# Reciprocal behind its guard, contiguous broadcast reads and a shorter lag in the query phase of a convolution, attention and expert-routing kernel

## The reference

```python
q = jax.nn.elu(q) + 1.0
k = jax.nn.elu(k) + 1.0
kv_cos = jnp.einsum('bshx,bshz->bhxz', k_cos, v)          # and kv_sin
qkv = jnp.einsum('bshx,bhxz->bshz', q_cos, kv_cos) + ...   # the same with sin
denom = 1.0 / (jnp.einsum('bshd,bhd->bsh', q_cos, k_cos.sum(axis=1)) + ... + 1e-05)
o = qkv * denom[..., None]
concat = o.reshape(b, s, h * d)
return concat @ dense_w.T + dense_b
```

## Time and profile before

| | us |
|---|---|
| median of three runs | 3816.84 |
| lowest, highest | 3796.03, 3817.02 |
| profiled execution | 3805.87 |
| its span | 3804.1 |
| PE busy | 3269.6 (86%) |
| DVE busy | 2955.0 (78%) |
| ACT busy | 1744.9 (46%) |
| POOL busy | 1609.1 (42%) |
| DVE idle until an `RB` load landed | 164.7 |

### The profile page before, as it was taken

One profiled execution on the slowest core, in us unless ns is written; L12 is line 12 of the kernel. 1 busy time (PEld: TensorE's weight loads), 2 busy tenths in 40 slices (PEclk: granted clock), 3 DMA queues, 4 the chain that ended last, 5 costly groups with the idle time before them and its releaser, 6 DMA issues.

```text
span 3804.1 us, 50603 instructions
## 1 busy us (share of the span) xinstructions
PE 3269.6 (86%) x16676; PEld 1503.9 (40%) x16676; DVE 2955.0 (78%) x3282; ACT 1744.9 (46%) x1880; POOL 1609.1 (42%) x1078
## 2 busy tenths in 40 slices
PE   4698888988898887988889888988889888998876
PEld 3343344433443334433444334433354334443353
DVE  6887977889787986879778896879878796758723
ACT  1166524764356533665247643565346642443210
POOL 1067712865147721676128650477217661210000
PEclk8899999999999998999999999999999999999967
DMA  1002640055201551025400552015510353106645
GB/s 51 18 1 60 136 98 27 1 119 119 65 19 27 132 119 44 1 65 132 96 27 1 119 118 65 19 25 133 119 44 1 79 126 89 32 1 138 138 124 214
DMA packets 154850, 279.55 MB, mean 73 GB/s; under 512 B 30285, under 2 KB 149613, under 8 KB 149677
## 3 DMA queue, kind: packets, MB, share of 16 engines
q1 hardware_dynamic: 154557, 275.89, 30.4%
HBM read 242.78 MB, written 33.05 MB: 73 GB/s over the span
## 4 chain that ended last, share of the span: by engine, by line
PE 46%; DVE 21%; DMA 14%; issue 9%; ACT 4%; SPq 3%; POOL 1%; DVEq 1%; ACTq 0%; POOLq 0%
DMA RB<-r_keep 10%; PE ps_C L1466 9%; PE ps_B L1451 5%; PE ps_A L1451 5%; PE ps_D L1466 4%; PE ps_E L1466 4%; DVE region L1112 4%; DMA r_keep<-RR 3%; DVE region L1104 3%; PE ps_D L1533 3%; DVE arena L930 3%; PE ps_D L1319 3%; PE ps_C L1533 2%; PE ps_E L1512 2%; DVE RR L1132 2%
## 5 line engine op out<-in xcount | busy, mean ns | idle before, releaser
L587 POOL TENSOR_TENSOR arena<-arena,UHL 128x896 f32<-128x896 f32 x525 | 1179.5, 2255 | 405.9 <-ACT UHL L719 404.1
L1112 DVE TENSOR_TENSOR region<-region,RB 128x896 f32<-128x896 f32 x448 | 615.9, 1375 | 165.2 <-DMA RB<-r_keep 164.7
L719 ACT ACTIVATE UHL<-arena,W8C 128x896 f32<-128x896 f32 x525 | 542.1, 1033 | 0.0
L565 POOL TENSOR_SCALAR ST<-ST 128x14 f32<-128x14 f32 x64 | 28.8, 449 | 1121.4 <-DVE ST L985 1119.5
L755 ACT ACTIVATE EQ<-ps_B,NEG 128x896 f32<-128x896 f32 x224 | 225.6, 1007 | 496.4 <-PE ps_B L1495 496.4
L1533 PE MATMUL ps_C<-region,small 128*128 128x448 f32 x896 | 408.5, 584 | 22.4 <-DVE region L1112 22.4
L1533 PE MATMUL ps_D<-region,small 128*128 128x448 f32 x896 | 395.8, 566 | 37.0 <-DVE region L1112 37.0
L597 POOL TENSOR_TENSOR UA<-region,CS 128x128 f32<-128x128 f32 (+1 forms) x400 | 229.4, 575 | 415.1 <-PE ps_C L1466 365.8
L1466 PE MATMUL ps_C<-region,UA 128*128 128x512 f32 (+1 forms) x800 | 378.4, 595 | 1.4 <-ACT region L653 1.3
L930 DVE SCALAR_TENSOR_TENSOR arena<-arena,W8C 128x448 f32<-128x448 f32 (+1 forms) x243 | 365.2, 1526 | 0.0
L755 ACT ACTIVATE EQ<-ps_A,NEG 128x896 f32<-128x896 f32 x224 | 225.4, 1006 | 270.5 <-PE ps_A L1495 270.5
(11 more groups left out here) (294 smaller groups left out, 5115.3 us busy)
## 6 DMA issues: line engine op xcount, KB each, us to landing
RB<-r_keep SPq DMA_DIRECT2D x448, 448.0 KB, 6.2
arena<-x SPq DMA_DIRECT2D x8, 1568.0 KB, 7.5
t_keep<-Y SPq DMA_DIRECT2D x7, 1568.0 KB, 5.2
r_keep<-RR SPq DMA_DIRECT2D x448, 7.0 KB, 2.1
w_keep<-region SPq DMA_DIRECT2D x7, 784.0 KB, 5.9
CST<-t_keep SPq DMA_DIRECT2D x2, 1568.0 KB, 9.8
small<-t_keep SPq DMA_DIRECT2D x2, 1568.0 KB, 13.3
plane<-w_keep SPq DMA_DIRECT2D x4, 784.0 KB, 16.1
```

Source lines behind the costliest of these rows:

```text
L587: pool.tensor_tensor(out=X[:, cut], in0=X[:, cut], in1=PRODUCT[m % 3], op=ALU.add).then_inc(pool_taps.sem, 1)
L719: act.activation(PRODUCT[m % 3].rearrange("p (h w) -> p h w", w=W), g_window(2 * g * ROWS + 2 * (k // 5), 2 * (k % 5) - 4, 2 * ROWS), ACT. ...
L1112: dve.tensor_tensor(out=q, in0=q, op=ALU.mult, in1=RB[:, cc].rearrange("p (c n) -> p c n", c=2)).then_inc(scaled.sem, 1)
```

## The change

Four edits, which all serve one ordering. `RECIP_LAG` goes from 6 to 5, so the reciprocal stands directly behind the guard. The lags of scaling, output, parts and fold each go down by one slot, and the slots of the second token norm with them; the phase has 69 slots instead of 70. The token transposes stand in even slots now, in which `ps_A` holds a projection, so they take `ps_B`. The columns of `SEL` are permuted so that the 16 rows of `r_keep` are kept by partition half (8 rows for i = 0, then 8 for i = 1), and each load then reads four neighbouring rows, one run of 7168 B per partition, where it read four runs of 1792 B.

```diff
-DEN_LAG, SUM_LAG, RECIP_LAG, RB_LAG, OUT_LAG, PARTS_LAG, FOLD_LAG = 4, 5, 6, 10, 11, 15, 20
+DEN_LAG, SUM_LAG, RECIP_LAG, RB_LAG, OUT_LAG, PARTS_LAG, FOLD_LAG = 4, 5, 5, 9, 10, 14, 19
...
-LN2_SLOTS = {29: 0, 45: 1, 61: 2, 69: 3}
-ALL_SLOTS = 70
+LN2_SLOTS = {28: 0, 44: 1, 60: 2, 68: 3}
+ALL_SLOTS = 69
...
-                uses += [(("yt2", LN2_SLOTS[j]), "A")] if j in LN2_SLOTS else []
+                uses += [(("yt2", LN2_SLOTS[j]), "BA"[j % 2])] if j in LN2_SLOTS else []
...
-                            at = HEADS * (s % 2) + 8 * h + i
-                            sp.dma_start(RB[HALVES[i], 2 * h:2 * h + 2, :].rearrange("p b (c n) -> p (b c) n", n=PIX),
+                            at = HEADS * (s % 2) + NCHUNK * i + 4 * h
+                            sp.dma_start(RB[HALVES[i], 2 * h:2 * h + 2, :].rearrange("p b n -> p (b n)"),
...
-                                                 [[0, C], [2 * PIX, 4], [1, PIX]]))\
+                                                 [[0, C], [1, 4 * PIX]]))\
...
-            link(dve.tensor_tensor(out=SEL[:, 0:HEADS].rearrange("p (g c h) -> p g c h", g=2, h=2),
+            link(dve.tensor_tensor(out=SEL[:, 0:HEADS].rearrange("p (h g c) -> p g c h", g=2, h=2),
```

## The result

The changed kernel is slower by half a per cent: 1.0055 of the time before, with an interval of 1.0044 to 1.0067. The medians are 3807.98 us before (15 runs, among them the three shown above) and 3826.9 after (15 runs). The ratio makes 17 to 26 us more, where the forecast was 3 us less than before. The profiled execution has a span of 3820.8 us against 3804.1, 16.7 more.

The account below looks back on a forecast made before the run. The DRAM loop of reciprocal, store, load and scaling was taken as the bound. Per turn +0.45 - 0.20 - 0.25 = 0.0; per pair +0.76 - 0.89 - 0.2 = -0.3, -3 us for 8 pairs: 3814, range 3762 to 3860.

Parts of the forecast that it names:

- The bound: Middle query step: the loop reciprocal, store, load, scaling, next reciprocal, 12.78 us, binds; DVE and PE aren't full.
- The intervals with the token norm: Four of 13 reciprocal intervals per pair, bound by DVE: guard's turn adds 0.76 us per pair, moved norm nothing.
- PE as the bound: Rival: PE waits 0.7 us per turn at the denominators' first half, +50 us, 3867; chance 0.17.
- The load: Loads of `RB` in the loop, longer runs: gain 0.2 us per turn, ends +0.25 and -0.4.
- The faster-load rival: Long runs bring a pair of `RB` loads 1 us sooner: -57 us in all, 3760; chance 0.23.
- The guard: On DVE it comes into the loop between scaling and reciprocal: +0.45 us per turn, lower end 0.26.
- The store: Stores of the reciprocals come through faster since half 1 loads start earlier: 0.25 us gained per turn, at worst nothing.
- First reciprocal and packets: Each pair's first reciprocal starts 0.89 us sooner; DMA packets fall by 86,016 if each run is one packet.
- Signs that were given for a wrong forecast: Landing under 5.6 us, a second L1512 wait in each turn, or token-norm intervals changing by more than 1 us.

Follow-up runs that it names:

- runs_only: Kernel before with the change's `SEL`, `r_keep` and loads (7168 B runs), old lags kept: 3781.83 us, -22 against before.
- scale_runs: Changed kernel with `RECIP_LAG` back at 6, so the reciprocal stands behind the second scaling of the step before: 3968.61 us, +164 against before.
- before_shortpool: Kernel before with each of POOL's convolution additions cut to 56 of 896 columns, rest of the sum left out: 3680.06 us, -123 against before.
- runs_only_den3: runs_only with PE's first half of the denominators one slot later: 3846.03 us, +39 against before.
- lags_only: Kernel before with the change's lags, slots and transposes' area, but old row order and 1792 B runs: 3863.88 us, +61 against before.
- recip_runs: runs_only with the reciprocal one slot up (slot 4s+5), all other lags as before: 3727.70 us, -77 against before.

## Why the prediction was wrong

**The bound: the failing step.** "Neither is full, the loop is the bound" took PE's 11.71 and DVE's 11.64 busy us as slack of one us in each, and DVE's wait of 1.14 as time that only a shorter loop would change. What the runs showed: with a shorter load the 3rd to 6th turns stay at 12.8 us, because the scaling grows by what the wait loses (0.95 + 1.38 before, 0.24 + 2.09 in runs_only). With a feature and a scaling more in the loop they go to 15.3 (scale_runs), and with POOL's additions shortened they fall to 12.4 (before_shortpool). A part of DVE's busy time is scalings of 2 us beside an addition that take 1.08 without one; it isn't a fixed amount of work that leaves slack. In the changed kernel the load's wait fell by 70 us, DVE's busy time grew by 39, and the sum over terms of the loop had neither.

**The intervals with the token norm: a term near nothing.** The sum gave the four intervals that don't wait for a load 0.76 us per pair, and to the token norm, moved with the lags, it gave "I count nothing". In the third pair these are the 7th, 8th, 10th and 11th. By the medians they changed by -0.9, +2.4, +0.3 and +1.7, together 3.4 us per looped pair before rounding, and some 24 for seven. That alone turns the forecast of 3 us less into a loss. In the 8th, L997 now stands ahead of a feature job that PE waits for. The distance that the prediction called kept is that of the transposes and their area; it didn't look at this part of the norm.

**PE as the bound: a rival that came true in part.** It put a wait of 0.7 us at the first half of the denominators into each of nine turns, 50 us in all. That half waits in three steps of a looped pair, by 1.08 to 1.23 us; its waits grew from 6.9 to 27.0 us in the whole kernel. The wait of 1.07 that the rival took from the earlier trace rows belongs to the second half, and those waits didn't grow (127.2 and 126.6). That moving the first half gives back 47 us is more than its own wait; the move also fills waits of the second.

**The load: sized too low.** 0.2 us per turn were taken, from a range up to 0.4; the landing of a load fell by 0.4, and by 0.5 in runs_only (6.2 to 5.7). The estimate of 0.2 to 0.3 us, worked out from the Trainium skill's "DMA: Bandwidth & Descriptors", section "Why small descriptors are slow (HBM only)", was for a pair of loads, and the landings lie above it. The reading that long runs are no faster where 64 partitions are the target is refuted. It rested on two rates from stretches that also hold other transfers. The prediction drew the same from the 8 of 16 ports that the Trainium skill, "SBUF — State Buffer", section "Door 1: The DMA port swizzle", gives partitions 0 to 63; that section says nothing of the length of a run, and no run here tests the ports. What the gain is worth depended on what else bound: 22 us in the old order, about 40 in the new lags, 53 with the loop open, 64 without the additions. The faster-load rival (3760) named the right mechanism and still gave too much, since in the old order half of the wait it removed (33 of 66 us) turned into longer scalings.

**The guard: nearly right in size, wrong in worth.** 0.45 was taken, 0.38 measured, and the 9 turns of 8 pairs would be 27 us; leaving it out gives 5 to 11.

**The store: not shown, and its mechanism didn't hold.** Store to load was forecast to go from 3.65 to about 3.4, because `den_parts` comes later. The means are 3.51 us before and 3.40 in the changed kernel. With the lags alone, where `den_parts` comes later too, it is 3.67; with the runs alone, where it doesn't, 3.15. So the lags lengthened it and the long runs shortened it.

**First reciprocal and packets: right.** 0.95 us earlier at the first reciprocal of the first pair, 0.89 forecast; 86,016 fewer packets, exactly.

**Signs that were given for a wrong forecast.** The norm intervals changed by more than 1 us, as one of them says. L1512 has a second wait in three steps of a pair, not in each turn. The landing stayed above 5.6 and didn't warn. Besides, L1112's DMA wait was to stay near 165 and fell to 95.

The measured time stands inside the range given, 3762 to 3860, and within 1% of before; the sign of the small difference was missed. That it came so near is luck: a cost of 40 to 61 us for the lags and a gain of 22 to 40 for the runs nearly cancelled, and the sum had both close to nothing.

**What stays open.** On top of the runs the lags cost about 40 us (runs_only to the changed kernel), and the move of one job gives some 47 back. But without POOL's additions the lags cost 70, and 40 remain with the job moved, so the account isn't closed by adding. Why the same move costs 60 us with the old lags isn't explained. That the middle scaling ends with POOL's addition is shown; what sets the time of that addition isn't: it starts when ACT's product is there, and ACT follows PE and DVE.

## What to carry to other kernels

Before a wait is called the bound, ask what the engine would do next if it ended: lengthen or shorten it, and see whether the turn moves or the wait only changes its name. When all lags of a pipelined schedule go down by one, each fixed job that isn't a lag (here PE's first half of the denominators, and the token norm's parts) changes its neighbours on every engine; look at which engines the reordered one now keeps waiting, most of all in the steps with extra work. To shorten a loop over DRAM, first take jobs out of it by order: moving the reciprocal ahead of the scaling and no other lag gave 24 us, and 77 with longer runs, where the whole shift of lags with the same runs lost 19.

## What the runs showed of the hardware that was not expected

- A scaling with two SBUF operands of 128x896 takes 1088 ns with POOL nearly idle, and 1375 to 1589 ns in the mean beside POOL's additions (before and runs_only_den3); single ones take up to 2.8 us in before and 4.1 in runs_only_den3.
- The first scaling of a middle step ended 0.94 to 0.95 us after a POOL addition did, in 31 of 35 cases in before and in 35 of 35 in runs_only, whether it had waited 0.95 or 0.24 us for its load.
- Loads of 448 KB into 64 partitions land in 6.2 us with runs of 1792 B (before, lags_only) and in 5.7 to 5.8 with runs of 7168 B (runs_only, the changed kernel).
- Stores of the reciprocals that are issued 0.8 us behind the last load before them take long: store to next load is 6.3 us in recip_runs, 3.15 in runs_only, where they are issued 3.8 to 4.1 us behind.
- After a wait of 2.77 us at L1512 the next output job of PE took 3.21 us, and after 3.59 us 3.35, instead of 1.77; the granted clock was 0.52 behind the first of these. So such a wait costs about 1.5 us more than itself. After waits of 1.1 to 1.35 us it took 1.77 in both kernels.
